# Adjacency loads of a graph kernel: 8 transfers of 64 partitions in place of 16 transfers of 32

## The reference

```
def _lap_mul(A, x):
    d = 1.0 / jnp.sqrt(jnp.sum(A, axis=-1))
    return d[:, None] * (A @ (d[:, None] * x))

h = relu(layernorm(x))
z = leaky_relu(_lap_mul(adj, h) @ W1 + b1, 0.1)
d2 = |z_i|^2 + |z_j|^2 - 2 z_i . z_j            # all pairs
S = exp(-sqrt(max(d2, 0) + 1e-10) / 2), kept for the 4 nearest of each row
x = x + _lap_mul(S + adj, h) @ W2 + b2
h = relu(layernorm(x))
x = x + h @ W_self.T + (adj @ h) @ W_neigh.T + b
```

## Time and profile before

| what | us |
|---|---|
| median of 3 executions | 1164.79 |
| lowest and highest of the 3 | 1163.4 and 1173.42 |
| the profiled execution, its own time | 1180.82 |
| its span, first to last instruction | 1178.8 |

### The profile page before, as it was taken

The page is one execution under the profiler, slowest core; times in us unless marked ns, Lnnn a source line. Parts: engine busy times, 40 slices in busy tenths (PEclk is TensorE's granted clock), DMA queues, the critical chain, the costliest instruction groups (busy, mean ns, idle before and its releaser), DMA issues.

```text
span 1178.8 us, 12596 instructions
## 1 busy us (share of the span) xinstructions
PE 929.5 (79%) x3378; PEld 583.5 (50%) x3378; DVE 868.9 (74%) x960; ACT 566.7 (48%) x1171; POOL 680.8 (58%) x1103
## 2 busy tenths in 40 slices
PE   0146437549559788769999999979989997999997
PEld 0023213224224333346766766435656645788886
DVE  2648558757768999747999998627687648888884
ACT  2454434545422221147777778424334433676763
POOL 9999988878673668104555565667777763000000
PEclk9987679689789888979999999999999998899999
DMA  9999999999999999739766767998989997699992
GB/s 210 293 315 321 330 331 363 341 335 359 361 333 358 339 313 356 296 125 367 260 250 247 256 235 270 395 412 316 349 299 356 371 341 269 248 369 383 376 387 90
DMA packets 98750, 369.10 MB, mean 313 GB/s; under 512 B 21264, under 2 KB 34320, under 8 KB 73872
## 3 DMA queue, kind: packets, MB, share of 16 engines
q1 hardware_dynamic: 51696, 258.43, 56.6%
q0 software_dynamic: 40960, 103.87, 30.7%
q10 hardware_dynamic: 6048, 6.29, 1.6%
HBM read 244.78 MB, written 123.73 MB: 313 GB/s over the span
## 4 chain that ended last, share of the span: by engine, by line
PE 41%; DVE 7%; POOL 5%; issue 4%; DMA 3%; ACT 2%; POOLq 0%; ACTq 0%; DVEq 0%
PE ps L1362 6%; PE ps L1380 5%; PE ps L1381 5%; PE ps L1382 5%; PE ps L1363 5%; PE ps L1364 5%; PE ps L1389 4%; POOL zt_lo L613 3%; PE ps L1359 2%; DVE araw_r L1207 2%; DVE araw L936 1%; DMA araw<-in_adj_dram 1%; DVE out_t L1164 1%; PE ps L1259 1%; PE ps L1271 1%
## 5 line engine op out<-in xcount | busy, mean ns | idle before, releaser
L389 POOL DMA_DIRECT2D araw<-in_adj_dram x704 | 382.7, 552 | 88.5 <-DVE tr L936 48.9
L1207 DVE TENSOR_TENSOR araw_r<-araw,tr_r 128x512 fp32r<-128x512 f32 (+1 forms) x184 | 213.9, 1220 | 63.4 <-ACT tr_r L815 63.3
L815 ACT ACTIVATE tr_r<-araw 128x2048 fp32r<-128x2048 f32 x88 | 166.3, 1910 | 74.4 <-DMA araw<-transposed 29.6
L613 POOL DMA_INDIRECT zt_lo<-neighbour_table,idx_st x128 | 144.2, 1126 | 48.8 <-issue 42.3
L761 ACT ACTIVATE araw<-ps,nsq 128x1024 f32<-128x1024 f32 x128 | 142.6, 1117 | 55.4 <-PE ps L1364 55.4
L1271 PE MATMUL ps<-tr,ys 128*128 128x512 f32 x256 | 130.7, 661 | 35.5 <-DVE ys L943 28.5
L659 ACT ACTIVATE ps<-araw 128x256 f32<-128x256 f32 x304 | 111.6, 367 | 81.9 <-DMA araw<-in_adj_dram 81.4
L936 DVE STREAM_TRANSPOSE tr<-araw 128x2048 f32<-128x2048 f32 x32 | 123.3, 3873 | 30.3 <-DMA araw<-in_adj_dram 26.7
L1389 PE MATMUL ps<-araw,ys 128*128 128x512 f32 x320 | 142.9, 602 | 2.6 <-ACT ys L806 2.6
L1362 PE MATMUL ps<-zt_lo,zs_hi 128*128 128x512 f32 x256 | 108.8, 425 | 0.0
L1066 DVE TENSOR_REDUCE bmax<-araw 128x64 f32<-128x4096 f32 x23 | 101.5, 4411 | 9.4 <-ACT araw L761 7.4
(11 more groups left out here) (164 smaller groups left out, 1460.7 us busy)
## 6 DMA issues: line engine op xcount, KB each, us to landing
araw<-transposed SPq DMA_DIRECT2D x128, 1024.0 KB, 7.1
araw<-in_adj_dram POOLq DMA_DIRECT2D x704, 128.0 KB, 16.2
keys_scratch<-araw SPq DMA_DIRECT2D x96, 512.0 KB, 3.5
transposed<-tr SPq DMA_DIRECT2D x32, 1024.0 KB, 8.6
transposed<-unit_zt_hi SPq DMA_DIRECT2D x8, 1024.0 KB, 9.3
transposed<-unit_zt_lo SPq DMA_DIRECT2D x8, 1024.0 KB, 8.7
transposed<-unit_sq_rows SPq DMA_DIRECT2D x8, 1024.0 KB, 9.5
transposed<-araw SPq DMA_DIRECT2D x8, 1024.0 KB, 5.3
```

The source lines that it names most:

```text
L389: gp.dma_start(araw[R * q:R * q + R, place, U * v:U * v + U], adj_v[q, :, g // 2, g % 2, v, :, c]).then_inc(a_first_in[place], DMA)
L613: gp.indirect_dma_start(out=gath[:, i, u, k, :], out_offset=None, in_=table, in_offset=bass.IndirectOffsetOnAxis(ap=idx_st[:, i, u * TOPK ...
L815: act.activation(ring_hi[:, place % TSLOTS], ring[:, j], ACT.Copy).then_inc(hi_done, 1)
L1207: ins = v.tensor_tensor(ring_lo[:, j, u], ring[:, j, u], ring_hi[:, place % TSLOTS, u].bitcast(F32), ALU.subtract)
```

## The change

A chunk is loaded by 8 transfers instead of 16: 4 row blocks v by 2 halves. Each writes 64 partitions (two column quarters), again 4 KB on each, 256 KB in all, from 256 runs of 1 KB. In the source pattern the two quarters are the outermost step, before the 128 rows. The count that readers wait for goes from 16 x 16 to 8 x 16.

```diff
-        PER_LOAD = QD * QD * DMA
+        PER_LOAD = 2 * QD * DMA
...
         def load_chunk(gp, g, c, place):
             for v in range(QD):
-                for q in (0, 2, 1, 3):
-                    gp.dma_start(araw[R * q:R * q + R, place, U * v:U * v + U],
-                                 adj_v[q, :, g // 2, g % 2, v, :, c]).then_inc(a_first_in[place], DMA)
+                for half in range(2):
+                    gp.dma_start(araw[2 * R * half:2 * R * half + 2 * R, place, U * v:U * v + U],
+                                 adj_v[2 * half:2 * half + 2, :, g // 2, g % 2, v, :, c]).then_inc(a_first_in[place], DMA)
```

## The result

The changed kernel takes 1958.88 us (median of 5, 1951.11 to 1971.56), beside 1166.92 us for the kernel before on the same chip (1163.4 to 1182.17). The ratio is 1.6734, interval 1.6654 to 1.6814: 67% slower, where 6.5% slower was forecast. The direction was right; the time lies far outside the range of 1145 to 1310. In the ratios and differences of this document, executions more than 1.5% above the fastest of the same kernel on the same chip are left out, for the kernel before too.

The account below looks back on a forecast made before the run. DMA was taken to bound the first phase. Loads at 68.3 engine-us per MB, 13.2 more, add 76 us to the profiled 1180.82: 1256.8, or 1240.8 as median, 6.5% slower; range for 8 in 10, 1145 to 1310.

Parts of the forecast that it names:

- what the first phase loses is lost by the whole, one for one: Adjacency loads, to about 474 us: any time the first phase gains or loses passes undiminished to the whole kernel.
- only two engines share a transfer: Split over the engines: source's outermost step of 2 leaves two engines a transfer, 128 KB each, bytes per engine unchanged.
- the 5 us named as the mark: Sign for two engines a transfer: minimum landing time rises from 2.8 to over 5 us; with sixteen it stays near 3.
- The forecast's +76 us: Load cost in the first phase: paired engines meet on the same partitions, mean 68.3 engine-us per MB, 13.2 more than before.
- Completion counts: Small packets of the loads: 16 a transfer, halved with 352 transfers, costed at nothing.
- no wait is added, and nothing queues behind a new one: Readers' waits on loads: on whole chunks before and after, so no added waiting; buffers and what frees them stay.
- The cover that I named for the issues: GpSimd's issue savings are hidden by the queue of loads waiting to land, 16.2 us median.
- Issues: GpSimd's load issues: 704 become 352 at 0.8 us each, 282 us in place of 388.6.
- Worth nothing to the sum: The 107 us GpSimd wins on issues add nothing, since the engines behind it are full.
- The rival "GpSimd becomes the bound": Load issues cost 1.25 us or more, deciding from 1.1 us: +51, 1216 us; at 2.05 us +250. Chance 0.14.
- if under 0.9 with GpSimd full, the issue is the bound: Sign in the first phase: DMA share should stay at 1.0; below 0.9 with GpSimd full, issuing limits.
- the side estimate of 65 us: By the skill page's 218 GB/s ceiling for one half, loads alone cost 73 engine-us per MB; sum some 65 us.

Follow-up runs that it names:

- run 10: The changed kernel, but GpSimd issues a chunk only when the chunk before it has landed: 2347.25 us, one run.
- run 2: Kernel before with its 16 transfers of 32 partitions, each reading 16 rows of two quarters, outermost step 2 (data misplaced): 1878.52 us, one run.
- run 3: The changed kernel with four transfers of 128 partitions, 512 KB each, four quarters outermost: 1449.64 us, ratio 1.2339 to the kernel before.
- run 4: Kernel before with quarters in the order 0, 1, 2, 3 instead of 0, 2, 1, 3: 1210.33 us, ratio 1.0312.
- run 11: The changed kernel with a semaphore of its own for each of a chunk's eight transfers: 1713.03 us, ratio 1.4566 to the kernel before.
- run 7: Kernel before with three small copies and waits on GpSimd after every fourth issue, slowing the pace of issues: 1283.57 us.
- run 8: Kernel before with the slowed pace of run 7, and each chunk issued only when the one before has landed: 1426.61 us, one run.
- run 9: Run 8 with one more wait for landings after 14 of a chunk's 16 transfers: 1513.4 us, one run beside 1188.76.
- run 5: Against the kernel before, four transfers of 128 partitions, 512 KB, each from 128 rows of one quarter, sixteen engines (data misplaced): 1145.22 us.
- run 1: Eight transfers of 64 partitions as in the changed kernel, but from 64 rows of one quarter, rows outermost (data misplaced): 1204.17 us, ratio 1.0256.
- run 12: Run 3 with a semaphore for each transfer: 1424.34 us, ratio 1.2003 to the kernel before.

## Why the prediction was wrong, and where it was right

*Right.* That what the first phase loses is lost by the whole, one for one: +774 us at the first distances, and 663 us for the rest in both. That only two engines share a transfer: the landing minimum went from 2.8 to 6.4 us, over the 5 us named as the mark, 528 packets a transfer come out with two carriers, and the lone transfer of run 10 has two packets at once. The Trainium skill's rule that I used ("DMA: Bandwidth & Descriptors", under "Why a DMA increments its semaphore by 16 and not by 1") is borne out by runs 2 and 3, with 2 and 4 carriers; the same section's line that on GpSimd's path all 16 engines post their count agrees with the 16 extra packets of each transfer. That the partitions written price a load is right in kind (run 4). The forecast's +76 us for it has a counterpart of +72 in the 4 KB packets, but that is luck in part: I had 76.6 engine-us per MB without stores and 40.3 under them, and the 4 KB packets cost 66 in stretches of 2 us without a store and 61 where stores take over half of the engines' time. That pairs meet is not shown.

*Wrong: "Completion counts", the small packets costed "at nothing".* This is the largest term of the engines' time. I multiplied the 16 small packets of the earlier trace rows by the number of transfers and took the fourteen idle engines to be free. They get 32 fillers each, and queue 0's cost rises from 55.1 to 0.58 x 16 x 1290 / 94.82 = 126 engine-us per MB, of which 62 are small packets; I had 68.3 in all. In time that is +359 us of small packets, put at nothing. As long as GpSimd stops it is not what the phase waits for (run 2); it becomes the limit when semaphores of their own shorten the stops (run 11). The rows of before could not show fillers, since all 16 engines carry there.

*Wrong: "no wait is added, and nothing queues behind a new one".* This is the step on which the measured time hangs: the chain of the first phase is issues and stops. No wait is in the code. But GpSimd has room for seven such transfers, 1.8 MB, and waits until the newest count of them is reached: 712.9 us at a releaser that the profile does not name. The cover that I named for the issues, the landing queue, was the very thing that the change shortened. Before, a transfer took 8 places on each list, so that some 120 would have fitted by the room found in run 2, and the buffers' waits came first.

*Wrong: "Issues".* 1.532 us each, inside my bounds (0.552 to 2.052) but not near the 0.8 taken: the duration goes by the runs that one engine gets, 8, 16, 32, 64 and 128 at 552, 617, 748, 1027 and 1532 ns. My ground against dear issues, a flat 552, was no evidence, since all 704 had the same 8. "Worth nothing to the sum" fell with it: run 7 prices the pace alone at +121, by estimate some 70 at the pace of the change.

*The rival "GpSimd becomes the bound"* named the place and the mark (from 1.1 us), and "if under 0.9 with GpSimd full, the issue is the bound" was the nearest to what was seen: 0.76 to 0.80. It was still not it: GpSimd is busy four tenths. It held idle time constant, and that is where the loss went. At 1.532 us its sum gives 539 + 85 us, some 625; the last issue came at 1252.6. Two sums of the prediction are also off in themselves, and nothing rested on them: at 2.05 us this rival's rule gives 722 + 85, so +333 and not +250, and the side estimate of 65 us comes to some 60 by its own working.

*What stays open.* Why small packets get long: a filler takes 11 ns alone and 28 after the change, a count 12 before and 256 after; what the long ones wait for is not shown, nor why the 4 KB packets go from 219 to 270 ns. How much of a landing, and so of a stop, is owed to the fillers and how much to the two carriers: the +121, +265 and +325 of runs 7 to 9 come from short transfers, and no run has two carriers without fillers. Why the lists hold what they hold: their room is read from 15 of 64 and 7 of 128 runs. Run 5 points at what would help, 128 partitions with 16 engines; no kernel here has that with the data in place, since a transfer of several quarters has them outermost.

## What to carry to other kernels

Before you merge transfers on GpSimd's queue, look at the outermost step of both patterns: if it is 2 or 4, as here, the merged transfer runs on as many engines, its issue costs by the runs that one of them gets, and all the others are sent as many packets that carry nothing. The Trainium skill's advice to coalesce small transfers ("DMA: Bandwidth & Descriptors", under "Rules for kernel authors") did not hold here by itself: with 16 carriers a quarter as many transfers were 1.4% faster (run 5) and half as many 2.6% slower (run 1), and the change, with half as many on two carriers, was 67% slower. When an issuing engine stands idle "until: issue" in a regular pattern, count the issues in a row and ask how many fit, and try semaphores of their own for the transfers in flight: it won 246 us where the engines had idle time, and some 30 where they had none (run 12).

## What the runs showed of the hardware

- Issue time on GpSimd by runs for one engine: 552 ns at 8, 617 at 16, 748 at 32, 1027 at 64, 1532 to 1556 at 128.
- From empty lists, room for 15 transfers of 64 runs for an engine and for 7 of 128, not for 16 and 8, and stops without a named releaser when it is used up.
- Room back only by the transfers' semaphore: GpSimd goes on 0.31 to 0.48 us after it has the counts of the newest transfer on it, at every such stop of the changed kernel and of runs 2, 3, 10 and 11. The same loads took 1958.88 us with one semaphore for eight and 1713.03 with eight semaphores.
- Fillers on engines that carry nothing: 528 packets for 256 KB with 2 carriers, 80 with 16. A filler has 16 bytes and takes 11 ns in a transfer that is alone, 28 in the mean after the change.
- TensorE's granted clock was 0.64 to 0.72 over the longer phase (0.73 to 0.90 before), so in the mean between its levels of 1.2 and 2.4 GHz, with long idle times between its matmuls; it has nothing to do with the loss, being busy 118 of 318 us at most.
